# A memory layer's state kept twice: updated by half-width products, its decay moved from TensorE to GpSimd

## What is computed

```python
for c0 in range(0, S, CHUNK):
    g = _grad_fn(W_state, k[:, sl], v[:, sl]) * GRAD_SCALE
    g = g * min(1 / norm(g), 1)
    def step(carry, xs):
        Sm = et * Sm - tt * gt
        Wm = (1 - at) * Wm + Sm
        return (Sm, Wm), Wm
    (S_state, W_state), Wtraj = scan(step, (S_state, W_state), xs)
    h = silu(q_t @ W1_t.T);  outs = h @ W2_t.T
out = rmsnorm(retrieved @ Wo.T) * norm_g * (hidden @ gW.T + gb)
x = layernorm(x + out)
# then each token goes to the expert with the best score, x + expert(x), and a second layernorm
```

## Time and profile before

| | us |
|---|---|
| median of 3 runs | 542.94 (542.05 to 548.37) |
| the profiled execution's own time | 546.91 |
| its span, first to last instruction | 545.6 |
| busy: TensorE | 451.0 |
| busy: VectorE | 386.4 |
| busy: GpSimd | 336.9 |
| busy: ScalarE | 305.5 |

### The profile page before, as it was taken

One profiled execution on the slowest core, in us unless ns is written; L12 is line 12 of the kernel. 1 busy time (PEld: TensorE's weight loads), 2 busy tenths in 40 slices (PEclk: granted clock), 3 DMA queues, 4 the chain that ended last, 5 costly groups with the idle time before them and its releaser, 6 DMA issues.

```text
span 545.6 us, 11167 instructions
## 1 busy us (share of the span) xinstructions
PE 451.0 (83%) x3506; PEld 342.4 (63%) x3506; DVE 386.4 (71%) x1146; ACT 305.5 (56%) x780; POOL 336.9 (62%) x451
## 2 busy tenths in 40 slices
PE   6595999999999989999997988975988685827662
PEld 4273777776776857768675856664757563716551
DVE  3658768898899988989779797887756463614322
ACT  2435167577577576677654766753765572415443
POOL 2004527449879778885787586763477766364556
PEclk9898699999999999999997999996999898777967
DMA  8442333453753646558453547387548645246511
GB/s 225 124 136 61 100 103 74 146 137 69 191 131 108 178 89 172 116 124 194 76 180 74 149 104 177 86 224 181 149 141 193 170 132 179 88 147 176 154 59 51
DMA packets 61354, 73.21 MB, mean 134 GB/s; under 512 B 17293, under 2 KB 48206, under 8 KB 61296
## 3 DMA queue, kind: packets, MB, share of 16 engines
q1 hardware_dynamic: 50624, 46.12, 31.2%
q0 software_dynamic: 8848, 25.44, 18.4%
q10 hardware_dynamic: 1824, 0.93, 0.7%
HBM read 44.19 MB, written 19.22 MB: 116 GB/s over the span
## 4 chain that ended last, share of the span: by engine, by line
PE 51%; DVE 14%; POOL 12%; issue 10%; ACT 7%; SPq 2%; another core or an unknown queue 2%; DMA 2%; POOLq 0%; DVEq 0%; ACTq 0%
PE bank L619 8%; PE bank L519 6%; PE bank L540 4%; PE both L1321 3%; PE bank L1321 3%; DVE kq_in L569 3%; POOL sorted_rows L1101 3%; POOL out L1367 2%; PE bank L971 2%; PE bank L1032 2%; ACT rows L1024 2%; DVE y L991 2%; SPq L1164 2%; PE both L930 2%
## 5 line engine op out<-in xcount | busy, mean ns | idle before, releaser
L1367 POOL DMA_INDIRECT out<-os,xs_token x71 | 70.9, 998 | 41.0 <-issue 17.1
L1101 POOL DMA_INDIRECT sorted_rows<-rows,index x64 | 74.7, 1167 | 24.6 <-issue 14.9
L569 DVE SCALAR_TENSOR_TENSOR kq_in<-shared,conv_w,kq_in 128x256 f32<-128x256 f32 x144 | 69.2, 535 | 13.7 <-ACT kq_in L560 13.6
L619 PE MATMUL bank<-front 128*128 128x256 f32 x256 | 65.4, 403 | 5.1 <-DVE bias_g L326 5.1
L1321 PE MATMUL bank<-shared,front 128*128 x212 | 55.3, 408 | 12.3 <-issue 5.7
L519 PE MATMUL bank<-front 128*64 128x256 f32 x512 | 61.3, 392 | 4.8 <-DMA front<-in_w_kv 4.8
L619 PEld LDWEIGHTS bank<-front 128*128 128x128 f32 x256 | 49.1, 201 | 13.8 <-DVE bias_g L326 5.4
L1321 PEld LDWEIGHTS bank<-shared,front 128*128 128x128 f32 x212 | 41.0, 203 | 20.7 <-issue 15.5
L519 PEld LDWEIGHTS bank<-front 128*64 128x64 f32 x512 | 37.1, 141 | 23.6 <-DMA front<-in_hidden_t 4.8
L1326 DVE BATCH_NORM_STATS2 st<-bank 128x6 f32<-128x256 f32 x53 | 20.2, 422 | 43.8 <-remote 23.2
L1024 ACT ACTIVATE rows<-y,rstd 128x256 f32<-128x256 f32 x64 | 34.3, 590 | 17.0 <-POOL rstd L1018 12.5
(11 more groups left out here) (214 smaller groups left out, 1230.4 us busy)
## 6 DMA issues: line engine op xcount, KB each, us to landing
front<-sorted_rows SPq DMA_DIRECT2D x71, 130.0 KB
front<-in_hidden_t SPq DMA_DIRECT2D x16, 512.0 KB
decay<-gate_clear SPq DMA_DIRECT2D x16, 512.0 KB
y<-in_hidden POOLq DMA_DIRECT2D x16, 512.0 KB
q<-kq_in SPq DMA_DIRECT2D x64, 64.0 KB, 2.5
carry<-carry_rows SPq DMA_DIRECT2D x32, 128.0 KB
hq<-hq SPq DMA_DIRECT2D x64, 64.0 KB
shared<-in_w_expert SPq DMA_DIRECT2D x2, 1024.0 KB
```

The lines of the kernel that those rows point to most:

```text
L569: dve.scalar_tensor_tensor(dst, raw[g][:, kind, :, tap:tap + P], conv_w[:, kind, tap:tap + 1], dst, ALU.mult, ALU.add))
L619: ins = pe.matmul(bank[:, (b % 2) * H:(b % 2 + 1) * H], xt[:, k, b * P:(b + 1) * P], w_g[:, k, :], start=k == 0, stop=k == KH - 1)
L1101: pool.indirect_dma_start(sorted_rows[:, :], bass.IndirectOffsetOnAxis(index[i2][:, b:b + 1], 0), R[:, b, :], None, bounds_check=NE * REGI ...
L1367: pool.indirect_dma_start(out[:, :], bass.IndirectOffsetOnAxis(xs_token[t % LOADS][:, i:i + 1], 0), os_[o][:, i, :], None, bounds_check=TO ...
```

## The change

The state is also kept in a second form, `kept[g]`: layer and row on the partitions (layer 1 on 0 to 63, layer 2 on 64 to 127), and W or S, batch and column on the free axis. In this form an update is one product for each batch and layer, into one half of the bank's partitions, with the factors on the gradient side; and the decay is elementwise: GpSimd computes `handed` = c S, `faded` = (a W, e S) in place, and `aged` = a W + c S. VectorE adds the bank to it (`state`). Then SyncE refills by DMA both `w12[g]` (four transfers instead of two) and `state[g]` (four, new). `ck` and `ch` are now the weighted gradients times the responses, and are computed behind `grad_w`, on GpSimd as before; `k_n` and `h` have three buffers; `g_dec`, `ident_g` and `end_c` are gone. All three rates come by way of `keep_rows` (one DMA more). At the start there are four loads and four zero fills for `kept`. The string `ORDER` is new throughout (each engine's instructions are issued in another order throughout).

```diff
-        keep_rows = nc.dram_tensor("keep_rows", [2, NB], F32).ap()
+        keep_rows = nc.dram_tensor("keep_rows", [2, 3, NB], F32).ap()
...
-        state = [sb(f"state{g}", [P, NB, 2, D]) for g in range(G)]
+        state = [sb(f"state{g}", [P, 2, NB, D]) for g in range(G)]
+        kept = [sb(f"kept{g}", [P, 2, NB, D]) for g in range(G)]
...
+        for g in range(G):
+            nc.sync.dma_start(kept[g][:, 0, :, :], dram["kept0"]).then_inc(s_kept, 16)
...
-        pool_const(diagonal(ident_g[:, 0, :], 0, [[-1, D]]))
-        pool.wait_ge(s_const, n_const)
-        pool_const(diagonal(ident_g[:, :, :], -D, [[0, 2], [-1, D]]))
...
         if updates(c):
-            sp.dma_start(keep_rows[i2].unsqueeze(1), keep_t[i2][NB:2 * NB, P - 1:P], allow_slow_non_contiguous=True).then_inc(s_short[i2], 16)
+            sp.dma_start(keep_rows[i2, 0:2].rearrange("w b -> (w b)").unsqueeze(1), carry_t[i2][:, P - 1:P], allow_slow_non_contiguous=True).then_inc(s_short[i2], 16)
+            sp.dma_start(keep_rows[i2, 2].unsqueeze(1), keep_t[i2][NB:2 * NB, P - 1:P], allow_slow_non_contiguous=True).then_inc(s_short[i2], 16)
...
-        mark("pool", n("end_c"), pool.tensor_scalar(ends[i2][:, 0, :], carry[i2][:, :, P - 1], 1.0, None, ALU.mult))
-        yield
-
-        dve.wait_ge(s_carry[i2], until(c, g, 3, 2))
-        wait("dve", n("end_c"), o2("upd_ps"))
-        mark("dve", n("g_dec"), dve.tensor_tensor(g_dec[i2][:, :, :, :], spread(ident_g[:, :, :].unsqueeze(1), 1, NB),
-                                                  spread(ends[i2].rearrange("p w b -> p b w").unsqueeze(3), 3, D), ALU.mult))
-
-        yield
-        who, wide_e = wide_engine(c, g)
-        wait(who, n("k_n"), n("scan_c"), o2("upd_ps"))
-        mark(who, n("ck"), wide_e.tensor_tensor(ck[i2][:, :, :, :], spread(k_n[i2][:, :, :].unsqueeze(2), 2, 2), at_end(i2), ALU.mult))
+        wait("pool", p("state"), o("aged"))
+        mark("pool", n("handed"), pool.tensor_tensor(handed[:, :, :], K0[:, 1, :, :], spread(from_w1.unsqueeze(2), 2, D), ALU.mult))
+        yield
+        wait("pool", n("handed"))
+        mark("pool", n("faded"), pool.tensor_tensor(K0[:, :, :, :], K0[:, :, :, :], spread(rates.unsqueeze(3), 3, D), ALU.mult))
+        yield
+        wait("pool", n("faded"))
+        mark("pool", n("aged"), pool.tensor_tensor(K0[:, 0, :, :], K0[:, 0, :, :], handed[:, :, :], ALU.add))
         yield
...
-        if updates(c):
-            who, wide_e = wide_engine(c, g)
-            wait(who, n("h"), o2("upd_ps"), n("scan_c"))
-            mark(who, n("ch"), wide_e.tensor_tensor(ch[i2][:, :, :, :], spread(h[:, :, :].unsqueeze(2), 2, 2), at_end(i2), ALU.mult))
-            yield
         wait("pool", n("inv_g"), f"theta0.{n_of(c, g) // 2}", o("grad_w"))
...
+        if not updates(c):
+            return
+        for name, scaled, of_grad in (("ck", ck, 0), ("ch", ch, 1)):
+            who, wide_e = wide_engine(c, g)
+            wait(who, n("grad_w"), n("scan_c"), o2("upd_ps"))
+            mark(who, n(name), wide_e.tensor_tensor(scaled[i2][:, :, :, :], spread(grad_w[i2][:, of_grad, :, :].unsqueeze(2), 2, 2), at_end(i2), ALU.mult))
+            yield
...
-            pe.matmul(ub, g_dec[i2][:, b].rearrange("p w d -> p (w d)"), ST[:, at].rearrange("p w d -> p (w d)"), start=True, stop=False)
-            pe.matmul(ub[:, 0:D], ck[i2][:, b].rearrange("p w d -> p (w d)"), grad_w[i2][:, 0, b, :], start=False, stop=False)
-            ins = pe.matmul(ub[:, D:P], ch[i2][:, b].rearrange("p w d -> p (w d)"), grad_w[i2][:, 1, b, :], start=False, stop=True)
+            pe.matmul(upd_of[0:D, :, b, :], k_n[n_of(c, g) % 3][:, b, :], ck[i2][:, b, :, :], start=True, stop=True)
+            ins = pe.matmul(upd_of[D:P, :, b, :], h_of[n_of(c, g) % 3][:, b, :], ch[i2][:, b, :, :], start=True, stop=True)
...
-        mark("act", n("state"), act.activation(ST[:, :, :, :].rearrange("p b w d -> p (b w d)"), upd[:, :], ACT.Copy))
+        wait("dve", n("upd_ps"), n("aged"))
+        mark("dve", n("state"), dve.tensor_tensor(K0[:, :, :, :].rearrange("p w b d -> p (w b d)"), K0[:, :, :, :].rearrange("p w b d -> p (w b d)"), upd[:, :], ALU.add))
...
         for side in range(2):
-            sp.dma_start(W12[half(side), :, :, half(side)].rearrange("p j w d -> p (j w) d"), ST[0:D, 2 * side:2 * side + 2, :, :].rearrange("p j w d -> p (j w) d")).then_inc(s_w12[g], 16)
+            for of in range(2):
+                sp.dma_start(W12[half(side), :, of, half(side)], K0[half(of), 0, side:NB:2, :]).then_inc(s_w12[g], 16)
+        for w in range(2):
+            for of in range(2):
+                sp.dma_start(ST[half(w), of, :, :], K0[half(of), w, :, :]).then_inc(s_state[g], 16)
...
+    for g in range(G):
+        pool.memset(kept[g][:, 1, :, :], 0.0).then_inc(s_zero, 1)
```

More of the change, by code:

```diff
@@ L380, in layers @@
     s_w12 = [sem(f"s_w12{g}") for g in range(G)]
+    s_state = [sem(f"s_state{g}") for g in range(G)]
     gt = [sb(f"gt{g}", [P, NB, H]) for g in range(G)]
@@ L390, in layers @@
     carry_t = two("carry_t", [2 * NB, P])
-    ends = two("ends", [P, 2, NB])
+    ends = two("ends", [P, 3, NB])
     theta = sb("theta", [P, 2, NB])
@@ L395, in layers @@
     carry = two("carry", [P, NB, P])
-    k_n = two("k_n", [P, NB, D])
+    k_n = [sb(f"k_n{i}", [P, NB, D]) for i in range(3)]
     kq = two("kq", [P, NB, P])
     ab_q = two("ab_q", [P, NB, P])
-    g_dec = two("g_dec", [P, NB, 2, D])
+    handed = sb("handed", [P, NB, D])
     ck = two("ck", [P, NB, 2, D])
@@ L403, in layers @@
     t_z = sb("t_z", [P, NB, D])
-    h = sb("h", [P, NB, D])
+    h_of = [sb(f"h{i}", [P, NB, D]) for i in range(3)]
     h_t = two("h_t", [P, 2, P])
@@ L663, in respond @@
         yield
-        wait("act", n("k_n_ps"), of_update(c, g, "ck"))
-        mark("act", n("k_n"), act.activation(k_n[i2][:, :, :].rearrange("p b d -> p (b d)"), bank[:, 0:2 * P], ACT.Copy))
+        wait("act", n("k_n_ps"), of_third(c, g, "upd_ps"))
+        mark("act", n("k_n"), act.activation(k_n[n_of(c, g) % 3][:, :, :].rearrange("p b d -> p (b d)"), bank[:, 0:2 * P], ACT.Copy))
         pro.freed_by(i, n("k_n"))
@@ L768, in learn @@
         yield
-        wait("dve", n("t_z"), of_update(c, g + 1, "ch"), o("h_ps"), o("sq_h"))
+        wait("dve", n("t_z"), of_third(c, g, "upd_ps"), o2("h_ps"), o2("sq_h"))
         mark("dve", n("h"), dve.scalar_tensor_tensor(wide(h[:, :, :]), wide(t_z[:, :, :]), 1.0, z, ALU.add, ALU.mult))
@@ L861, in retrieve @@
         C = resp[i2][:, 0]
-        ST, W12, W2_T = state[g], w12[g], w2_t[g]
+        ST, W12, W2_T, K0 = state[g], w12[g], w2_t[g], kept[g]
         i, bank = grab(rtv, n("zq"))
+        if c:
+            pe.wait_ge(s_state[g], c * 64)
         wait("pe", n("grad_w"), n("kq0"), n("kq1"), n("ab_q"))
@@ L869, in retrieve @@
             for side in range(2):
-                pe.matmul(bank[half(side), columns], ST[:, 2 * side + j, 0, :], ab_q[i2][:, 2 * j + side, :], start=True, stop=False)
+                pe.matmul(bank[half(side), columns], ST[:, 0, 2 * j + side, :], ab_q[i2][:, 2 * j + side, :], start=True, stop=False)
             for side in range(2):
@@ L911, in retrieve @@
             for side in range(2):
-                pe.matmul(bank[half(side), j * P:(j + 1) * P], ST[:, 2 * side + j, 1, :], ab_h[:, 2 * j + side, :], start=True, stop=False)
+                pe.matmul(bank[half(side), j * P:(j + 1) * P], ST[:, 1, 2 * j + side, :], ab_h[:, 2 * j + side, :], start=True, stop=False)
             for side in range(2):
@@ L952, in retrieve @@
         yield
+        if c == 0 and g == 0:
+            all_ready(act)
         wait("act", n("w2_ps"), n("dh_ps"))
```

132 lines of the change are left out of this document (69 added, 63 removed).

## The result

The changed kernel takes 559.21 us (median of 6 runs, 552.08 to 560.88), the kernel before, measured beside it, 546.75 (542.05 to 551.20): a ratio of 1.028, interval 1.023 to 1.033. A ratio here compares the fast executions of both kernels alone; by it the change costs 15 us, by the two medians 12.5. The forecast was 8 us faster, and the result lies outside the range of 521 to 551. A second measurement of the two gave 1.022 (1.013 to 1.031).

The account below looks back on a forecast made before the run. TensorE was taken as the bound (95% busy from 75 to 350 us), VectorE close behind at 87%. Terms -13.4 -0.9 -0.4 +4.4 +2.7 +1.0 -0.7 -1.0 gave -8.3 us, from the median 542.94 to 535; range 521 to 551.

Parts of the forecast that it names:

- The products: TensorE's update products: 0.95 us instead of 2.62, 1.67 saved each, eight of twelve on the path, 13.4 us off.
- rival (d): Update products on TensorE: the halves do not run side by side, 0.7 saved each; 543; chance 0.17 together with rival (b).
- Decay on GpSimd, queue: GpSimd's three new decay steps: 2.35 us per update, 22.7 us more in all, at weight 0.19, 4.4 us on.
- The hold: GpSimd's wide decay steps hold VectorE for 8 us, a third of it on the path: 2.7 us on.
- SyncE's queue: Refill transfers: eight issues instead of two and one keep transfer, 4.0 us more per update, mostly hidden: 1.0 us on.
- Copy and swap: ScalarE's twelve bank copies go, 0.9 us off; VectorE swaps building the decay matrix for the addition, 0.4 off.
- rival (b): VectorE's in-order queue frees the update's bank 0.7 us later each time: 8.4 on, 543; chance 0.17 with rival (d).
- Moved steps: `ck` and `ch` behind `grad_w` on GpSimd: 22 us cover two products of 1.1 us, so no cost.
- The new sequence: The new issue order of all engines: no work changed, bounded by 8 us either way, taken as 1 us off.
- The start: Two GpSimd steps on `ident_g` go, ahead of everything that waits for the constants: 0.7 us off.
- Rival (c): GpSimd's decay steps hold VectorE in every group: all 28.2 us on the path against 15.4 off; 556; chance 0.15.
- Rival (a): TensorE's saved time comes back whole, GpSimd's three decay steps fitting into its idle time: 524; chance 0.24.

Follow-up runs that it names:

- the repeat: The changed kernel unaltered, measured a second time beside the kernel before: 556.93 us, ratio 1.022.
- e7: Kernel before with both gradient products of each batch left out, only the decay product kept: ratio 0.988 to the kernel before.
- m4: n1 with the eight products of each update issued twice, same result: ratio 0.997 to the kernel before, against 1.002 for n1.
- e1: Changed kernel with GpSimd's three decay steps replaced by one-column fills, decay left out: ratio 1.015 to the kernel before.
- e2: Changed kernel with the decay steps replaced by fills about as long, which read nothing, decay left out: ratio 1.013 to the kernel before.
- e4: Changed kernel without the four transfers that refill `state`, which stays at its first value: ratio 1.031 to the kernel before.
- h3: Kernel before with eight transfers for each update instead of two, four going to a spare place: ratio 1.014 to the kernel before.
- n1: Changed kernel with decay (tiny fills instead) and addition left out, the bank copied to `kept` by ScalarE: ratio 1.002 to the kernel before.
- m2: n1 with two refill transfers of the old shape instead of eight, so `state` is not refilled: ratio 0.990 to the kernel before.
- h2: Kernel before with the twelve copies of the bank on VectorE instead of ScalarE: ratio 1.013 to the kernel before.
- h1: Kernel before, old order, with `ck` and `ch` computed behind `grad_w`: ratio 1.019 to the kernel before.
- m5: n1 with `ck` and `ch` computed for the first two updates alone, left out in the other ten: ratio 0.995 to the kernel before.
- m6: Kernel before with `ck` and `ch` computed for the first two updates alone, left out in the other ten: ratio 0.997 to the kernel before.
- e3: The changed kernel's work issued in the sequence of the kernel before, with `k_n` in four buffers: ratio 1.041 to the kernel before.
- p2: Changed kernel, decay on GpSimd, with four of the eight transfers made by ScalarE as copies: ratio 1.035 to the kernel before.
- p1: Changed kernel with the decay on VectorE and four of the eight transfers made by ScalarE as copies: ratio 1.022 to the kernel before.

## Why the prediction was wrong

Taken in the order of its sum:

- **The products: right at full clock alone, and their worth wrong.** 0.95 us was forecast. TensorE's timeline at the first update of the changed kernel:

```profile
73.43 0.27 PE L942 MATMUL both<-ck,k_n 128*64 128x128 f32 x1
73.44 0.27 PE L943 MATMUL both<-ch,h 128*64 128x128 f32 x1
...
74.40 1.78 PE L624 MATMUL bank<-front 128*128 128x256 f32 x7
```

  From its first record to its successor it takes 0.97 us, and the records run in pairs, so the halves do go side by side: rival (d) is out. But this is one update. The windows view of TensorE for the first and for the last one (busy, granted clock, DMA share, GB/s):

```profile
73.43:74.40 0.97, 0.97 (x20) 1.00 1.06 366
...
335.34:337.20 1.86, 1.86 (x18) 0.50 0.96 368
```

  At a granted clock of 0.50, the lower of the two levels (1.2 GHz), the same products take twice as long. Four of the twelve updates ran so (from 189.7, 221.1, 288.5 and 335.3 us) and the one from 140.3 in part; three others were followed by a wait for VectorE. From the first product to the next work the twelve take 19.2 us (19.4 in the repeat), 32.3 before: **13.1 us saved and not 20.0**. The prediction priced them all at full clock.

  The step "I take 8: 8 x 1.67 = 13.4 us off" failed by this and by its weight. Alone in the kernel before, taking out about as much as was forecast is worth 6.4 us (e7), and beside the rest of the change none that can be measured (m4, where decay and addition are left out). A line's share of the chain says where the chain lay, not what is won: VectorE, at 87%, was next, as the prediction noted ("not a whole one") but did not price.
- **Decay on GpSimd, queue: size a little low, worth about right.** 2.75 us for an update (2.35 forecast; the sum of two full operands, `aged`, took 0.82 and `handed` 0.80, not 0.62). The forecast of 4.4 us on the path stands beside 3.7 at the milestone from e1 to e2 and nothing in their ratios.
- **The hold: undersized by some three times.** "I put a third of it on the path ... 2.7 on". VectorE was held for 10 to 12 us more (8 forecast), and e2 against the changed kernel shows 8 to 10 us at the milestone and, with e4 in the changed kernel's place, 9 in the ratios. The second factor, the share on the path, was the bigger fault.
- **SyncE's queue: 1.0 forecast, 6 to 8 without the decay on GpSimd** (h3, n1 to m2), none visible with it (e4).
- **Copy and swap: 1.3 off forecast.** The addition did run unheld in all twelve cases, but work added to VectorE's queue cost 6.8 us in the kernel before (h2). The mechanism is rival (b)'s; its 8.4 was near.
- **Moved steps: nothing forecast.** "22 us cover two GpSimd products" looked only at the update behind them, and not at what VectorE does at that moment. In the old sequence the move costs 10 us (h1); in the new one it lies between nothing and some 8 us (m5, m6). In the changed kernel `ck` waits 6.0 us in three cases for `grad_w`.
- **The new sequence: 1.0 off.** Its worth is not shown: 1% between e3 and e4, with intervals that overlap and four transfers less in e4.
- **The start: 0.7 off forecast.** The first update came 2.4 to 3.2 us earlier, but in e7 and m6, which are the kernel before up to there, it came at 73.4 and 74.0 too. So no run shows a gain of the start.

With 6 for 13.4, 9 for 2.7 and 6 for 1.0 the forecast of -8.3 becomes +10, against 12.5 measured. That is not a proof: with h2's 6.8 on for the 1.3 off it would be +18, and the costs do not add. Alone, h1, h2 and h3 come to 4.5%, the decay to some 1.6% (e1 to e4), and all of them together with the saving to 2.2 to 2.8. Each edit's wait lies partly beside another's.

Rival (c), the hold, was the right mechanism, and had a chance of 0.15. That its time (556) is nearly right is luck: it set 28.2 us of hold and queueing against 15.4 off, both twice what the runs showed or more. Its threshold, 15.4 us of hold and queueing, was a sum against the full gain of TensorE. The decay cost 12 to 14 us at the milestone, less than that, but with a gain of 6 or less it was enough. Rival (a), all of TensorE's time back, is out by the idle time in the stretch. Of the signs listed, VectorE's means in L574 and `onehot` rose as said (493 to 550), the clock fell under 0.95, TensorE was at 88% of the stretch and not at 92 to 93%, and eight of the twelve updates took over 1.5 us from their first product to the next work.

What stays open: the addition's own cost in the new sequence, how much of h1's cost the new sequence absorbs, and why the granted clock was at its lower level in those updates.

## What to carry to other kernels

Before work is taken from the busiest engine and given to another, ask what the second-busiest one will feel: here, with VectorE at 87%, the time taken from TensorE became idle time. Price GpSimd steps that read SBUF also at the time for which VectorE stands behind them, and not at GpSimd's own weight alone; between the full time of the hold (e2) and a part of it (m5) only a run decides. If VectorE can do them in two thirds of the time, try them there: it was worth 1.2% here (p2 to p1). Look at all instances of a smaller product and not at the first, since some may run at the lower clock. A chain's share bounds what an engine's microsecond can give and does not forecast it; leaving the work out in one run (as e7) measures it.

## What the runs showed of the hardware that was not expected

- **Fills do not hold VectorE.** The hold theory of e2 had this; the prediction did not have it. GpSimd fills of 480 to 700 columns, 29 us in all, left the convolution at 570 ns, where reading steps of about that length made it 651. Its median in the whole span is 474 to 475 ns in the kernel before, in the changed one and in e1: the hold is in a few long instances (up to 3.3 us).
- **The expert stage has two speeds.** The kernel before took 547.5 us in one measurement and 519.3 in another on one and the same chip. So it does not go with the chip, as the expectation for the repeat took it. In the profiles the time after the milestone is 67 to 71 us in all six kernels at the level of 519 and 82 to 92 in all fourteen at the other (68.2 in e1, 85.4 in n1). From the expert stage's first statistics on VectorE (388.4 in e1, 391.4 in n1) to the milestone it is 66.2 against 70.5 us, so the slower stage also delays the end of the chunks. The windows view of TensorE (busy, clock, DMA share, GB/s), n1 first, then e1, shows the same clock and more moved:

```profile
450.00:500.00 50.00, 35.26 (x184) 0.86 0.49 155
```

```profile
450.00:500.00 50.00, 41.19 (x217) 0.86 0.62 192
```

  Whether the transfers are the cause, and what makes the stage faster at one time than at another, is not shown here. It moves the ratio too: 15 us lost in the chunks are a larger share of 519 than of 547.
- **Less work came with a lower clock.** The granted clock over the stretch was 0.99 before and 0.94 after, with TensorE idle for 33 us of it instead of 13; in e7, idle for 26 us, it was still 0.98. The amount of idle time does not order the runs: n1, idle for 26 us as well, was granted 0.93, and m2, idle for 25, 0.96. It cost time where it struck: four updates of the changed kernel took 1.8 to 1.9 us instead of 1.0.
